# Pool's row transfers in the attention: tied to ScalarE's steps, and the scatter at six a step

## The chip, the cores and the metric

The kernel runs on one core of a Trainium2 chip. The metric is the device time of one execution in microseconds, as the median of several runs. The core's engines each follow their own queue of instructions and meet at semaphores: TensorE (PE), VectorE (DVE), ScalarE (ACT), GpSimd (POOL) and SyncE (SP). Transfers by DMA are issued from SP's, ScalarE's and Pool's queues; only Pool issues those that take their row numbers from a tile (indirect transfers).

## The reference

A "macaron" block on x of 16 x 256 tokens, 128 wide, in float32:

```
x = x + 0.5 * ffn(layernorm(x))
x = x + attention(layernorm(x))        # 16 heads of 64, causal, softmax
x = x + 0.5 * ffn(layernorm(x))

ffn(h): scores = sigmoid(h @ gate_w.T)           # 64 experts
        the best 4 of 8 groups by their two best biased scores; the best 8 experts in them
        weights = scores of the 8 / their sum * 2.5
        y = sum over the 8 experts of weight * (silu(h @ We_gate) * (h @ We_up)) @ We_down
        y + (silu(h @ Ws_gate) * (h @ Ws_up)) @ Ws_down     # shared expert
```

Both feed-forward blocks use the same weights. An expert is 64 wide.

## The kernel before

The 4096 tokens are 8 chunks of 512 (four tiles of 128 tokens each). x stays on the chip in `x_all`. In each feed-forward block four chunks are *dense*: every expert pair is computed for all 512 tokens (33 slots a chunk, lines 824, 828 and 840), and the products are weighted with zero for the experts not chosen; SP spreads the weights (`f_mix_wide`). The other four chunks are *sparse*. Their normalised tokens (`xk`) are written by Pool to rows of the DRAM tensor `x_rows`, sorted by expert: for each of 16 token tiles and each of the 8 choices one indirect transfer of 128 rows (`dispatch`, line 488), 128 transfers in all, each counting `scattered` up by 16. SP then loads groups of four tiles of `x_rows` (`load`, line 742), TensorE turns and multiplies them with the tile's own expert (`quads`: lines 582, 607, 616 and 636), and SP stores the results to `y_rows`. Later Pool fetches for each token tile its 8 lists of result rows (`gather`, line 524, 128 transfers), and VectorE adds them with their weights to `x_all` (line 542).

The program is three blocks of code, one after another on every engine: `ffn_first`, `attention`, `ffn_second`. A block opens when all engines have ended the one before.

`attention` runs 64 steps (16 rows of 256 tokens, four heads a step) and three slots behind them. In slot k TensorE projects q, k and v of step k, while step k-1 goes through the softmax: ScalarE's slot is the exponentials of step k-1 in two pairs (`exp_done` counts pairs), the copies of q (line 1361) and k (line 1377, `k_read`), the three copies of the turned probabilities (line 1386, `probT_done`), then the copy of v. VectorE's slot is the copy of o (line 1496), the normalising of both pairs (lines 1482 and 1487), from time to time the normalising of a row (line 1004), three adds of gathered rows, the maxima of the two pairs (lines 1504, 1505 and 1508; the exponentials wait for line 1508), and between the two maxima up to four steps of the second block's routing, planning and placing. So the attention also holds the gathers and adds of the first block (three lists a step, steps 0 to 42, the add four steps behind its gather) and the front of the second block: the row numbers of its four sparse chunks are placed in steps 48 to 51, and from step 49 on Pool issues half a tile's lists, four transfers, a step. Pool waits in the attention for the row numbers (`idx_done`), for a free buffer before a tile's first gather (`added`), and for the moments of a row before its small pair of instructions that make `rstd` (`rstd_of`, lines 1018 and 1021; `front_rstd`, lines 1557 and 1562). It waits for no step as such.

`ffn_second` starts with the first dense chunk on TensorE, beside it Pool issues what is left of the scatter, now with a small memset behind each transfer (`b.space`, line 143). Then come the sparse groups and then the other three dense chunks. In `quads` the first load waits for all of `scattered`, and so does Pool's first copy of high expert weights (`copy_high`, line 727):

```python
        def load(i):
            if i == 0:
                sp.wait_ge(r.scattered, 16 * TOPK * CT * SPARSE)
            if i >= 3:
                sp.wait_ge(turned, SPARSE + i - 2)
            sp.dma_start(q.xq[:, i % 3, :, :], rows(x_rows, i)).then_inc(loaded[i % 3], 16)
```

The first four groups (`j < SPARSE`) are the shared expert of the sparse chunks and need no load. Ahead of the loads SP's queue has the spreads of the first dense chunk and of the first two groups of the next, and the store of the first dense chunk (`store_x`, line 2102), which waits for that chunk's update of x (line 909).

Of the kernel before, what the change touches and what calls it, by code (L numbers as in the profile page):

```python
# [16 lines left out]
P = 128  # L17
# [4 lines left out]
TOPK = 8  # L22
# [3 lines left out]
H = 16  # L26
HD = 64
SEQ = 256
CT = 4
# [13 lines left out]
SPARSE = 4  # L43
# [8 lines left out]
HALVES = (range(0, TOPK // 2), range(TOPK // 2, TOPK))  # L52
# [96 lines left out]
def router(ctx, nc, tag, order, w, x_all, b, x_rows, f):  # L149
# [13 lines left out]
    idx_done, scattered = sem("idx_done"), sem("scattered")  # L163
# [307 lines left out]
    def on_gpsimd(pool):  # L471
        veps, moments, rstd = b.veps, b.moments, b.rstd

        def rstd_of(r):
            pool.wait_ge(ln_step, LN_STEPS * r.front + 2)
            nc.gpsimd.tensor_tensor(veps[:, :], moments[:, :, 1], w["eps"][:, 0:CT], ALU.add).then_inc(rstd_step, 1)
            pool.wait_ge(rstd_step, 2 * r.front + 1)
            if r.front >= 1:
                pool.wait_ge(ln_step, LN_STEPS * r.front)
            nc.gpsimd.tensor_tensor(rstd[:, :], veps[:, :], w["minus_half"][:, :], ALU.pow).then_inc(rstd_step, 1)  # L480

        def dispatch(i, spaced=True):
            tile, half = divmod(i, 2)
            k, t = divmod(tile, CT)
            if t == 0 and half == 0:
                pool.wait_ge(idx_done, k + 1)
            for j in HALVES[half]:
                nc.gpsimd.indirect_dma_start(  # L488
                    x_rows[:, :], bass.IndirectOffsetOnAxis(ap=b.idx[:, f, CT * k + t, j:j + 1], axis=0),
                    b.xk[:, k, t, :], None).then_inc(scattered, 16)  # L490
                if spaced:
                    b.space(pool)

        return rstd_of, dispatch
# [537 lines left out]

A_ROUTE, A_COUNT, A_PLAN, A_RANK, A_DISPATCH = 14, 44, 45, 48, 49
A_HEAD, A_MIX = 47, 55
GATHER_STEP, ADD_LAG = 3, 4

def attention(nc, w, x_all, banks, psum, rows, b, mix_rows, y_rows, first, second, gathered, added):
# [16 lines left out]
    with ExitStack() as ctx:  # L1055
# [61 lines left out]
        def lists_of(k):  # L1117
            return range(max(GATHER_STEP * k, 0), min(max(GATHER_STEP * (k + 1), 0), SPARSE * CT * TOPK))
# [430 lines left out]
        @block.gpsimd  # L1549
        def _(pool):  # L1550
            rstd_of = rows.on_gpsimd(pool)
            _, dispatch = second.on_gpsimd(pool)
            gather = comb.on_gpsimd(pool)

            def front_rstd(b_):
                pool.wait_ge(c_ln, LN_STEPS * b_ + 2)
                nc.gpsimd.tensor_tensor(b.veps[:, 0:TB], b.moments[:, 0:TB, 1], w["eps"][:, 0:TB], ALU.add)\
                    .then_inc(c_rstd, 1)
                pool.wait_ge(c_rstd, 2 * b_ + 1)
                if b_ >= 1:  # L1560
                    pool.wait_ge(c_ln, LN_STEPS * b_)
                nc.gpsimd.tensor_tensor(b.rstd[:, 0:TB], b.veps[:, 0:TB], w["minus_half"][:, 0:TB], ALU.pow)\
                    .then_inc(c_rstd, 1)

            for k in range(STEPS):
                for i in lists_of(k):
                    gather(i // TOPK, (i % TOPK,), spaced=False)
                if k >= A_DISPATCH:
                    dispatch(k - A_DISPATCH, spaced=False)
                if front_row(k, 6) is not None:  # L1570
                    front_rstd(front_row(k, 6))
                if moments_row(k) is not None:
                    rstd_of(moments_row(k))
# [49 lines left out]
def ffn_first(nc, w, x_all, psum, b, mix_rows, x_rows, y_rows, zero, r, rows, x, dr):  # L1623
# [6 lines left out]
    with ExitStack() as ctx:  # L1630
# [189 lines left out]
        def _(pool):  # L1820
# [35 lines left out]
            for i, slot_ in enumerate(SCATTER_AT):  # L1856
                while waiting and FIRST_AT[waiting[0].n] < slot_:
                    rstd_of(waiting.pop(0))
                if i == 0:
                    pool.wait_ge(zeroed, 16 * len(CLEAR_AT))  # L1860
                dispatch(i)
            copy_high = qd.on_gpsimd(pool)
            pool.wait_ge(dn.x_updated, DENSE)
            for i in range(QUADS_R):
# [76 lines left out]
def ffn_second(nc, w, x_all, psum, b, mix_rows, x_rows, y_rows, r, out, dispatched, gathered, added):  # L1941
# [5 lines left out]
    with ExitStack() as ctx:  # L1947
# [126 lines left out]
        @block.gpsimd  # L2074
        def _(pool):
            rstd_of, dispatch = r.on_gpsimd(pool)
            gather = comb.on_gpsimd(pool)
            for i in range(dispatched, 2 * SPARSE * CT):
                if i == dispatched + 3:
                    rstd_of(in_dense[0])  # L2080
                dispatch(i)
            copy_high = qd.on_gpsimd(pool)
            for i in range(QUADS_R):
                copy_high(i)
                if i == Q_AT + 1 - SPARSE:
                    rstd_of(among)
            for side in range(YBUFS):
                pool.wait_ge(qd.y_stored[side], 16 * len(range(side, QUADS_R, YBUFS)))
            last = (2 * (SECOND_AT[7] - C_FROM)) // 11 + 2
            for t in range(SPARSE * CT):  # L2090
                if t == last:
                    rstd_of(in_dense[1])
                gather(t)
# [30 lines left out]
def macaron(nc, x, P_q, P_k, P_v, P_o, gate_w, gate_bias, We_gate, We_up, We_down, Ws_gate, Ws_up, Ws_down, out):  # L2124
    B, M, _ = x.shape
    tiles = B * M // P
# [8 lines left out]
    with ExitStack() as ctx:  # L2135
# [20 lines left out]
        with ExitStack() as early:  # L2156
# [5 lines left out]
            with nc.sbuf_tensor("zero", [P, CHUNK], F32) as zero:  # L2162
                ffn_first(nc, w, x_all, psum, b, mix_rows, x_rows, y_rows, zero, first, rows, x_v, dr)
            attention(nc, w, x_all, banks, psum, rows, b, mix_rows, y_rows, first, second, gathered, added)
        ffn_second(nc, w, x_all, psum, b, mix_rows, x_rows, y_rows, second, out_v, tiles // (SEQ // P) * (H // 4) - A_DISPATCH,
                   gathered, added)

# [21 lines left out]
```

## Time and profile before

| | |
|---|---|
| median of 3 runs | 1611.32 us (1610.64 to 1612.96) |
| the profiled execution's own time | 1613.64 us |
| its span in the profile | 1611.9 us |
| TensorE busy | 1528.5 us, 95% |
| VectorE busy | 1166.3 us, 72% |
| ScalarE busy | 766.3 us, 48% |
| Pool busy | 722.5 us, 45% |
| scatters, line 488 | 256, 1033 ns each |
| gathers of the attention, line 524 | 128, 977 ns each |

The span is what the hardware profiler recorded on the core; the execution's own time is a little longer. Busy shares are means over stages of different kinds; what bounds a stage is read from the waits in it. In the trace's rows the times are microseconds from the start of the span; a queue's name with a small q (SPq) is the issuing of a transfer, not its data.

### The profile page before, as it was taken

The page shows a single profiled execution, that of the slowest core. Times are in us where ns is not written, and L with a number is a line of the kernel's source. Part 1 is how long each engine was busy: PE and PEld are TensorE (multiplying, and loading weights), DVE is VectorE, ACT ScalarE, POOL GpSimd, SP SyncE. Part 2 cuts the span into 40 slices and gives each one's busy share as a digit, 9 for nine tenths or more (in the row PEclk, how much of TensorE's full clock was granted, in tenths as well). Part 3 has the DMA queues.
Part 4 walks back from the last instruction along what each step waited for, and adds up shares of the span by engine and source line. Part 5 has one row for each costly group of instructions (what it writes and reads, how often), then busy time and mean ns, then how long its engine had stood idle before and what let it go on. Part 6 is the DMA issues. An engine that isn't in the chain of part 4 may idle for free. (4 is left out here: it accounts for less than half of the span.)

```text
span 1611.9 us, 27350 instructions
## 1 busy us (share of the span) xinstructions
PE 1528.5 (95%) x8683; PEld 971.2 (60%) x8683; DVE 1166.3 (72%) x3354; ACT 766.3 (48%) x2105; POOL 722.5 (45%) x1123
## 2 busy tenths in 40 slices
PE   5899999999999899999999998999997999999998
PEld 2344444444788677777777776775446885444443
DVE  4698888765444588989898988765875845768675
ACT  2234223222455577777777776774224552222222
POOL 1000088888222344333334105443883225878730
PEclk9999999999999899999999999999998999999999
DMA  9999655553687111000000001103464884666652
GB/s 184 206 259 249 156 127 140 131 142 93 176 223 206 48 28 28 21 21 21 26 21 24 11 2 38 37 31 92 125 157 135 228 224 112 147 149 146 136 132 65
DMA packets 202043, 181.31 MB, mean 112 GB/s; under 512 B 39408, under 2 KB 154288, under 8 KB 201904
## 3 DMA queue, kind: packets, MB, share of 16 engines
q1 hardware_dynamic: 175056, 132.34, 34.8%
q0 software_dynamic: 16384, 33.59, 7.7%
q10 hardware_dynamic: 10464, 13.63, 2.5%
q8 instruction: 74, 1.21, 0.3%
q14 instruction: 65, 0.53, 0.1%
HBM read 121.83 MB, written 57.67 MB: 111 GB/s over the span
## 5 line engine op out<-in xcount | busy, mean ns | idle before, releaser
L868 ACT ACTIVATE f_hid<-banks 128x512 f32<-128x512 f32 (+1 forms) x264 | 157.6, 597 | 511.6 <-PE banks L828 511.5
L488 POOL DMA_INDIRECT x_rows<-r_xk,r_idx x256 | 264.4, 1033 | 138.6 <-issue 53.3
L890 DVE TENSOR_TENSOR f_hid<-banks,f_hid 128x512 f32<-128x512 f32 (+1 forms) x264 | 181.5, 687 | 145.1 <-ACT f_hid L868 144.9
L840 PE MATMUL banks<-f_hid,wd 128*128 128x512 f32 x528 | 273.3, 601 | 12.5 <-DVE f_hid L903 12.5
L824 PE MATMUL banks<-r_xT_d,gu 128*128 128x512 f32 x528 | 276.4, 605 | 4.7 <-DMA wd<-in_L_ffn_We_down 3.1
L828 PE MATMUL banks<-r_xT_d,gu 128*128 128x512 f32 x528 | 273.5, 600 | 0.0
L903 DVE TENSOR_TENSOR f_hid<-f_mix_wide,f_hid 128x512 f32<-128x512 f32 x256 | 176.0, 687 | 31.9 <-DMA f_mix_wide<-mix_rows 29.5
L840 PEld LDWEIGHTS banks<-f_hid,wd 128*128 128x128 f32 x528 | 99.6, 192 | 146.3 <-issue 120.9
L828 PEld LDWEIGHTS banks<-r_xT_d,gu 128*128 128x128 f32 x528 | 100.8, 191 | 130.1 <-issue 126.5
L824 PEld LDWEIGHTS banks<-r_xT_d,gu 128*128 128x128 f32 x528 | 97.5, 192 | 120.3 <-issue 110.6
L524 POOL DMA_INDIRECT a_g<-y_rows,r_idx x128 | 125.1, 977 | 66.3 <-issue 35.2
L1386 ACT COPY a_probT<-banks 128x512 f32<-128x512 f32 x192 | 106.2, 588 | 101.9 <-PE banks L1249 101.0
L524 POOL DMA_INDIRECT f_g<-y_rows,r_idx x128 | 128.9, 1007 | 41.2 <-issue 20.2
L1487 DVE TENSOR_SCALAR a_prob<-a_prob,a_inv 128x128 f32<-128x128 f32 (+1 forms) x512 | 130.8, 323 | 4.5
L1351 ACT ACTIVATE a_prob<-banks,a_bias 128x256 f32<-128x256 f32 x256 | 127.7, 499 | 0.0
L1228 PE MATMUL banks<-a_kT,a_qT 64*128 64x128 f32 (+1 forms) x1024 | 119.3, 351 | 0.0
L1348 ACT ACTIVATE a_prob<-banks,a_bias 128x128 f32<-128x128 f32 x256 | 99.6, 389 | 30.6 <-DVE a_bias L1508 30.5
L1249 PE MATMUL banks<-ident,a_prob 128*128 128x128 f32 x768 | 106.1, 275 | 2.5 <-ACT a_qT L1361 2.1
L143 POOL MEMSET r_spare<- 128x256 f32 x324 | 106.6, 329 | 0.2
L1264 PE MATMUL banks<-a_probT,a_v 128*64 128x256 f32 (+1 forms) x1024 | 97.3, 332 | 1.5 <-ACT a_probT L1386 0.3
L1249 PEld LDWEIGHTS banks<-ident,a_prob 128*128 128x128 f32 x768 | 89.4, 142 | 12.4 <-issue 3.5
L1504 DVE TENSOR_REDUCE a_top<-banks 128x2 f32<-128x256 f32 x128 | 53.4, 417 | 59.2 <-PE banks L1232 58.4
(243 smaller groups left out, 2879.5 us busy)
## 6 DMA issues: line engine op xcount, KB each, us to landing
f_mix_wide<-mix_rows SPq DMA_DIRECT2D x124, 512.0 KB
x_rows<-zero ACTq DMA_DIRECT2D x12, 1024.0 KB, 5.9
f1q_xq<-x_rows SPq DMA_DIRECT2D x48, 256.0 KB, 3.2
y_rows<-f1q_yq SPq DMA_DIRECT2D x48, 256.0 KB, 2.5
f2q_xq<-x_rows SPq DMA_DIRECT2D x48, 256.0 KB, 3.4
y_rows<-f2q_yq SPq DMA_DIRECT2D x48, 256.0 KB, 2.8
x_rows<-r_xk,r_idx POOLq DMA_INDIRECT x256
wd<-in_L_ffn_We_down SPq DMA_DIRECT2D x7, 512.0 KB, 10.8
```

Of the source, the lines that this page charges most:

```text
L488: nc.gpsimd.indirect_dma_start(x_rows[:, :], bass.IndirectOffsetOnAxis(ap=b.idx[:, f, CT * k + t, j:j + 1], axis=0), b.xk[:, k, t, :], Non ...
L524: nc.gpsimd.indirect_dma_start(g_buf[:, t % GBUFS, j, :], None, y_rows[:, :], bass.IndirectOffsetOnAxis(ap=b.idx[:, f, t, j:j + 1], axis=0 ...
L824: nc.tensor.matmul(gate_bank[g % 3][0:rows, :], w["gu"][:, 0, experts, :].rearrange("p e f -> p (e f)"), x, start=True, stop=True)
L828: nc.tensor.matmul(up_bank[g % 3][0:rows, :], w["gu"][:, 1, experts, :].rearrange("p e f -> p (e f)"), x, start=True, stop=True).then_inc( ...
L840: mm = nc.tensor.matmul(acc[:, :], w["wd"][0:rows, 2 * p, :], d.hid[0:rows, g % HIDS, :], start=(p == 0), stop=(p == PAIRS))
L868: nc.scalar.activation(d.hid[0:rows, g % HIDS, :], gate_bank[g % 3][0:rows, :], ACT.Silu)\
L890: nc.vector.tensor_tensor(d.hid[0:rows, g % HIDS, :], up_bank[g % 3][0:rows, :], d.hid[0:rows, g % HIDS, :], ALU.mult).then_inc(gated, 1)
L903: nc.vector.tensor_tensor(d.hid[:, g % HIDS, :], d.mix_wide[:, n % 2, p % SPREAD, :], d.hid[:, g % HIDS, :], ALU.mult).then_inc(weighted, 1)
L1228: nc.tensor.matmul(scores[pair][h][:, cols], qT[side_rows, i, pair, rows_q], kT[side_rows, i, pair, cols_k], start=(cols.start == 0), stop ...
L1249: mm = nc.tensor.transpose(bank[:, j * P:(j + 1) * P], prob[:, n * P:(n + 1) * P], w["ident"][:, :])
L1351: e = nc.scalar.activation(prob[:, o + P:o + NPB], scores[pair][h][:, P:NPB], ACT.Exp, bias=bias[:, i, pair, 1, h:h + 1], scale=HD ** -0.5 ...
L1487: m = nc.vector.tensor_scalar(prob[:, a:b], prob[:, a:b], inv[:, i, pair, late, h:h + 1], None, ALU.mult)
```

## The change

The unit of `dispatch` becomes one list (one transfer) instead of half a tile. In the attention, each step of Pool gets three points, and Pool waits at each of them for a place in ScalarE's work (`reach`, from step 1 on): at the first for the first pair's exponentials of step k-1, at the second for the copy of k of step k, at the third for the last probability copy of step k-1. Behind each point it issues one gather (steps 0 to 42) or two scatter transfers (from step 49 on). The scatter thus has six transfers a step, 90 in the attention's 15 steps instead of 60, and `ffn_second` begins at list 90 with 38 left, where it had 68. The small `rstd` instructions stay behind the step's transfers. The order of the 128 transfers, the spacing memset outside the attention and the place of `rstd_of` after twelve transfers in `ffn_second` stay as they were. The first block's calls are rewritten for the new unit and do the same.

```diff
-        def dispatch(i, spaced=True):
-            tile, half = divmod(i, 2)
-            k, t = divmod(tile, CT)
-            if t == 0 and half == 0:
-                pool.wait_ge(idx_done, k + 1)
-            for j in HALVES[half]:
+        def dispatch(lists, spaced=True):
+            for i in lists:
+                tile, j = divmod(i, TOPK)
+                k, t = divmod(tile, CT)
+                if t == 0 and j == 0:
+                    pool.wait_ge(idx_done, k + 1)
                 nc.gpsimd.indirect_dma_start(
...
-GATHER_STEP, ADD_LAG = 3, 4
+GATHER_STEP, SCATTER_STEP, ADD_LAG = 3, 6, 4
...
+            def reach(k, part):
+                if k < 1:
+                    return
+                if part == 0:
+                    pool.wait_ge(exp_done, 2 * k - 1)
+                elif part == 1:
+                    pool.wait_ge(k_read, k + 1)
+                else:
+                    pool.wait_ge(probT_done, 3 * k)
+
             for k in range(STEPS):
-                for i in lists_of(k):
-                    gather(i // TOPK, (i % TOPK,), spaced=False)
-                if k >= A_DISPATCH:
-                    dispatch(k - A_DISPATCH, spaced=False)
+                fetched = lists_of(k)
+                for part in range(GATHER_STEP):
+                    reach(k, part)
+                    for i in fetched[part:part + 1]:
+                        gather(i // TOPK, (i % TOPK,), spaced=False)
+                    if k >= A_DISPATCH:
+                        m = SCATTER_STEP * (k - A_DISPATCH) + 2 * part
+                        dispatch(range(m, m + 2), spaced=False)
...
-            for i in range(dispatched, 2 * SPARSE * CT):
-                if i == dispatched + 3:
-                    rstd_of(in_dense[0])
-                dispatch(i)
+            dispatch(range(dispatched, dispatched + 12))
+            rstd_of(in_dense[0])
+            dispatch(range(dispatched + 12, TOPK * SPARSE * CT))
```

## Rows read from the trace of the kernel before

**Rows 1.** The page's chain that ended last, shares of the span by line.
```profile
PE banks L824 5%; PE banks L828 5%; PE banks L840 5%; POOL x_rows L488 4%; PE banks L607 3%; PE banks L636 2%; PE banks L582 2%; POOL r_spare L143 1%; PE banks L616 1%; DVE f_hid L890 0%; DVE f_hid L903 0%; DVE x_all L542 0%; DMA f2q_xq<-x_rows 0%; DMA x_rows<-r_xk,r_idx 0%; DVE x_all L909 0%
```

**Rows 2.** The chain near 1214 us: start, duration, what.
```profile
1213.70 2.28 DMA x_rows<-r_xk,r_idx
...
1215.99 2.92 DMA f2q_xq<-x_rows
```

**Rows 3.** Timeline of Pool: start, duration, what, idle time before it and its releaser.
```profile
1067.30 0.96 POOL L488 DMA_INDIRECT x_rows<-r_xk,r_idx  x1 [0.30 <-issue]
1068.57 0.96 POOL L488 DMA_INDIRECT x_rows<-r_xk,r_idx  x1 [0.30 <-issue]
1110.66 0.96 POOL L488 DMA_INDIRECT x_rows<-r_xk,r_idx  x1 [41.13 <-POOLq L1055]
...
1213.70 0.96 POOL L488 DMA_INDIRECT x_rows<-r_xk,r_idx  x1 [0.17 <-issue]
```

**Rows 4.** Timeline of TensorE around the first loaded group.
```profile
1208.80 0.71 PE L636 MATMUL banks<-wd,f2q_hidT 64*128 64x128 f32 x8
1218.95 1.11 PE L582 MATMUL banks<-ident,f2q_xq 128*128 128x128 f32 x4 [9.44 <-DMA f2q_xq<-x_rows]
...
1223.29 1.11 PE L582 MATMUL banks<-ident,f2q_xq 128*128 128x128 f32 x4
...
1226.18 0.66 PE L582 MATMUL banks<-ident,f2q_xq 128*128 128x128 f32 x4
...
1228.52 0.66 PE L582 MATMUL banks<-ident,f2q_xq 128*128 128x128 f32 x4
```

**Rows 5.** Windows: length, busy PE, PEld, DVE, ACT, POOL, granted clock, DMA share, GB/s.
```profile
1204.00:1206.00 2.00, 1.76 (x16) 1.53 (x15) 0.83 (x2) 1.24 (x3) 1.83 (x4) 1.00 1.00 274
...
1218.00:1220.00 2.00, 1.05 (x5) 1.05 (x6) 0.00 (x0) 0.00 (x0) 1.10 (x5) 0.50 1.00 287
```

**Rows 6.** Windows of whole steps, line 1508 alone: length, DVE busy, count, clock, DMA.
```profile
635.41:778.46 143.05, 5.89 (x32) 1.00 0.09 23
1000.98:1068.07 67.09, 3.29 (x16) 1.00 0.14 43
1068.07:1101.80 33.73, 1.36 (x8) 1.00 0.02 6
```

**Rows 7.** Line 1508, all of it: ns least/median/most; who waited (us, times).
```profile
L1508 DVE TENSOR_SCALAR a_bias<-a_top x128: 169/170/405, 537.7 to 1099.9; 128x4 f32<-128x4 f32 x128
...
  ACT a_prob L1348: 30.5, 21
```

**Rows 8.** Timeline of SP's queue.
```profile
1204.26 0.37 SPq L2102 DMA_DIRECT2D out<-x_all  x1
```

**Rows 9.** Tile f2q_xq, 1200 to 1240 us: its loads.
```profile
DMA to landing us min/median/max: 2.7/3.0/4.3
```

**Rows 10.** Timelines of Pool, ScalarE and VectorE in steps 55 to 57.
```profile
1028.07 0.19 POOL L1018 TENSOR_TENSOR n_veps<-n_moments,eps 128x2 f32<-128x2 f32 x1 [14.24 <-DVE n_moments L997]
...
1029.25 1.03 POOL L488 DMA_INDIRECT x_rows<-r_xk,r_idx  x1 [0.20 <-issue]
...
1029.51 1.07 ACT L1386 COPY a_probT<-banks 128x512 f32<-128x512 f32 x2 [1.03 <-PE banks L1249]
...
1044.20 0.58 DVE L1004 TENSOR_SCALAR n_xn<-x_all,n_moments,n_rstd 128x128 f32<-128x128 f32 x2
```

**Rows 11.** Windows of the same whole steps, line 1487 alone.
```profile
635.41:778.46 143.05, 32.51 (x129) 1.00 0.09 23
1000.98:1068.07 67.09, 16.51 (x64) 1.00 0.14 43
1068.07:1101.80 33.73, 8.09 (x33) 1.00 0.02 6
```

**Rows 12.** Timelines of ScalarE and VectorE in step 57.
```profile
1040.91 0.24 ACT L1351 ACTIVATION_READ_ACCUMULATOR a_prob<-banks,a_bias 128x1 f32 x1
...
1042.04 1.05 DVE L1487 TENSOR_SCALAR a_prob<-a_prob,a_inv 128x128 f32<-128x128 f32 x4
```

More of the change, by code:

```diff
@@ L1860, in _ @@
                     pool.wait_ge(zeroed, 16 * len(CLEAR_AT))
-                dispatch(i)
+                dispatch(range(4 * i, 4 * i + 4))
             copy_high = qd.on_gpsimd(pool)
@@ L2077, in _ @@
             gather = comb.on_gpsimd(pool)
-            for i in range(dispatched, 2 * SPARSE * CT):
-                if i == dispatched + 3:
-                    rstd_of(in_dense[0])
-                dispatch(i)
+            dispatch(range(dispatched, dispatched + 12))
+            rstd_of(in_dense[0])
+            dispatch(range(dispatched + 12, TOPK * SPARSE * CT))
             copy_high = qd.on_gpsimd(pool)
@@ L2164, in macaron @@
             attention(nc, w, x_all, banks, psum, rows, b, mix_rows, y_rows, first, second, gathered, added)
-        ffn_second(nc, w, x_all, psum, b, mix_rows, x_rows, y_rows, second, out_v, tiles // (SEQ // P) * (H // 4) - A_DISPATCH,
+        ffn_second(nc, w, x_all, psum, b, mix_rows, x_rows, y_rows, second, out_v, SCATTER_STEP * (tiles // (SEQ // P) * (H // 4) - A_DISPATCH),
                    gathered, added)
```

## The prediction

> **What bounds the kernel now.** I read four views: the page's chain of work that ended last, then that chain inside the start of the second sparse block, then the timelines of TensorE, SP and Pool around the place it named, and last the attention in stretches of whole steps.
>
> The chain is mostly TensorE, but 4% of the span is Pool's scatter line and 1% the memset that spaces the transfers [rows 1]: a place where TensorE is not the bound. There the chain runs along Pool's scatters to the last one at 1213.70, then 2.28 us until the last one has landed, then 2.92 us for the first load of the scattered rows [rows 2]. Pool's own queue shows how it came to that: in the attention its last transfer starts at 1068.57; then it idles for 41.13 us until the next block of code opens, issues the rest from 1110.66 on, and is done with the last at 1213.70 + 0.96 = 1214.66 [rows 3]. TensorE has finished the first dense chunk and the four shared-expert groups at 1208.80 + 0.71 = 1209.51 and waits 9.44 us for the load [rows 4]. It then starts at the lower clock level: the granted clock of that stretch is 0.50 of 2.4 GHz, after 9 us in which it did nothing [rows 5]. Groups of four tiles start at 1218.95, 1223.29, 1226.18 and 1228.52 [rows 4], that is 4.34, 2.89, then 2.34 us; 2.34 is the pace that the later ones keep. So the late scatter costs 9.44 + (4.34 - 2.34) + (2.89 - 2.34) = **12.0 us** of the end. From the first group on TensorE sets the pace, and what follows is laid out by group and slot: a gain here is carried to the end.
>
> In the attention no single engine sets all steps. Two instructions of line 1508 are one step, so the three stretches are 16, 8 and 4 steps [rows 6]: 143.05/16 = 8.94 us with gathers and the first block's adds, 67.09/8 = 8.39 us while Pool issues scatters nearly without a break, 33.73/4 = 8.43 us with Pool idle. In the first kind VectorE has a part: ScalarE waited 30.5 us in 21 places for line 1508 [rows 7].
>
> **Scatter six a step.** 15 steps (49 to 63) issue 6 instead of 4 transfers: 90 instead of 60, and 38 instead of 68 stay for the second block. The 68 and one pair of small instructions took 1214.66 - 1110.66 = 104.0 us [rows 3]; with some 1.4 us for that pair, 102.6/68 = 1.51 us each. 38 take 57.4 + 1.4 = 59 us: done at about 1169.5, landed 2.3 us later, 45 us earlier than before and 38 us before TensorE wants the rows. That wait is gone.
>
> What is late next: the first load. On SP it stands behind the store of the first dense chunk, issued at 1204.26 in 0.37 us when that chunk's update has ended [rows 8]. The load can be issued at 1204.7. Such loads land after 2.7 to 4.3 us [rows 9]: at 1207.4 to 1209.0. TensorE is ready at 1209.51, so it has 0.5 to 2.1 us in hand. I take no rest of the stall, and no drop of the clock, since TensorE has work until then. If the store, in a stretch where the DMA engines are already fully busy [rows 5], takes 1 us more than the 4.3, the rest is 0.5 us; both ends go into the range as 0 to 1.5.
>
> Cost in the attention: 6 transfers at 1.27 us (the pace of the attention's last two [rows 3]) are 7.6 us of an 8.4 us step; a pair of rstd instructions each fourth step, 1.2 us from its start to the next transfer [rows 10], makes it 7.9 on average. If a step falls behind, the next wait is already met and Pool catches up, because the thresholds only rise. The last pair goes out in step 63, and three more slots of the loop follow before the block closes. The four extra steps filled (60 to 63) are no dearer by the rows: 8.39 us with Pool busy against 8.43 with it idle [rows 6]. Price 0; the ends are below, with the hold.
>
> **Three points per step.** Before, only the small rstd instructions held Pool; transfers ran in bursts. Now step k's first transfer waits for the first pair's exponentials, the second for ScalarE's copy of k, the third for the last probability copy. Three things can come of it.
>
> (a) Later gathers. A tile's last gather goes at the first point of step f+3 at the latest, its first add is in step f+4: over 8 us for a transfer of 1 us plus some 2.3 us to land. Nothing waits. The wait for a free buffer, which Pool met in bursts, is met two steps ahead. Price 0; behind a late gather VectorE would hold all maxima and so ScalarE, but one step of cover would first have to be lost.
>
> (b) Later rstd. The small pair is queued behind step k's third point and its transfers. Before it ran as soon as the moments were there. In step 55 it started at 1028.07, and its reader, line 1004, ran at 1044.20 [rows 10]. The third point of that step is the end of the probability copies at 1029.51 + 1.07 = 1030.6 [rows 10]; two transfers add 2.5, the pair 1.2: 1034.3, with 10 us in hand. Price 0.
>
> (c) Contention between Pool's transfers and VectorE. Line 1487 (eight a step) took 32.51/129 = 252 ns each with gathers, 16.51/64 = 258 with scatters and 8.09/33 = 245 with Pool idle [rows 11]; line 1508 5.89/32 = 184, 3.29/16 = 206 and 1.36/8 = 170 [rows 6], at most 405 [rows 7]. With gathers that is 8 x 7 + 2 x 14 = 84 ns a step, 3.6 us over the 43 gather steps. The new points move this. In step 57 the first pair's exponentials end at 1040.91 + 0.24 = 1041.15; a transfer from there ends near 1042.15, and line 1487 starts at 1042.04, after copying o [rows 12]: an overlap of 0.1 us. The other two I place from the order of the code alone: after the copy of k VectorE is ending its second group of 1487, and after the last probability copy it is in the maxima or in routing, where most of its instructions are of other kinds. So single gathers mostly miss the sensitive instructions, and I take 0.7 us of the 3.6 back. Bounds: all back, -3.6; or one collision a step at line 1508's worst, 43 x (405 - 170) ns = +10.1. The nearest rows, eight steps full of scatters at the same 8.4 us, speak for a value near zero.
>
> A rule of the Trainium skill ("SBUF — State Buffer", Who interferes with whom) speaks against this edit: a tensor_scalar in its two-port mode and a GpSimd instruction exclude each other for the whole instruction, and the one that comes second stands still. The first point puts a transfer just ahead of line 1487. By that rule the sum would be the 1618 us of the lock rival below; [rows 6, 11] show only 7 to 36 ns of it per instruction, and by them it is 1598.6.
>
> **Sum.** Against the profiled execution: 1613.64 - 12.0 - 0.7 = 1600.9. That execution lies 2.3 us above the median of the runs, so 1611.3 - 12.7 = **1598.6 us**.
>
> **Rivals.**
> - *Lock.* Each of VectorE's groups of 1487 that starts just behind a transfer loses half of its 0.95 us. Of 43 gather steps all have one such start: 43 x 0.45 = 19 us, and it is slower than before: 1598.6 + 19 = 1618. For it: the point is fixed relative to VectorE's work, so a hit would be repeated each step, and in steps where VectorE is behind (21 waits of ScalarE) it counts in full. Against: the mean of 258 ns under solid scatters. It decides from 12.7 us on, 0.3 us a step. Chance 0.10.
> - *The load is late anyway.* SP's load, store and the spread before them collide at 1204 to 1206, the load lands at 1211, TensorE waits 2 us and starts again at the lower clock, for up to 2.5 us more: 1598.6 + 4.5 = 1603. For it: DMA share 1.00 there. Against: 38 us without scatters ahead, and 0.5 us in hand even at 4.3. Chance 0.15.
> - *The hold helps.* All contention goes and VectorE's late steps get shorter: 3.6 us and perhaps as much again, where a short delay also moved a wait: 1592 to 1596. Chance 0.10.
> - *Nothing gained.* The scatters are not the last cause of the 9.44 us; SP or the index lists are. Then 1611. Against: the load is issued 2.3 us after the last scatter starts, and SP had been idle since 1204.6. Chance 0.03.
> - *The forecast*: 1596 to 1602, chance 0.62.
>
> **From these.** Range 1592.5 to 1606: it takes in the forecast, the late load, the hold that helps, and an attention dearer by up to 7 us; it leaves out the rest of the lock's cases, no gain, and unforeseen ones. 0.2% is 3.2 us, about what a measurement can tell from no change. Faster: 0.62 + 0.15 + 0.10 + 0.01 of the lock = 0.88; same 0.05; slower 0.07.
>
> **What the profile after would show.** 90 scatters before the block closes, 38 behind it, ended near 1170; Pool idle from there until the high-weight copies; TensorE's wait of 9.44 gone and clock 1.0 through the first groups, 2.34 us apart from the first loaded one; gathers of the attention three a step, evenly; line 1487 at 245 to 258 ns; steps of 8.9 and 8.4 us as before. The prediction is wrong if line 1487 or 1508 has a new mean in the gather steps, if line 1004 waits for Pool, or if the load lands after TensorE is ready.

## The result, and the profile after

The changed kernel took 1599.68 us (median of 4 runs, 1596.78 to 1600.90), the kernel before beside it 1612.14 (4 runs, 1610.64 to 1615.26): a ratio of 0.9917, 95% interval 0.9896 to 0.9938. Forecast were 1598.6 and a range of 1592.5 to 1606. The profiled execution's span fell from 1611.9 to 1598.2 us.

The page's chain that ended last no longer goes through Pool or a DMA (answers to [rows 1]):

```profile
PE banks L824 6%; PE banks L828 6%; PE banks L840 6%; PE banks L607 3%; PE banks L636 2%; PE banks L582 2%; PE banks L616 1%; DVE f_hid L890 1%; DVE f_hid L903 1%; DVE x_all L542 0%; DVE r_eqt L450 0%; PE banks L188 0%; ACT f_hid L868 0%; PE banks L849 0%; DVE r_chosen L344 0%
```

Pool's timeline (answers to [rows 2, 3]): the attention's last transfer, the first of the 38 behind it, and the first copy of high weights, which waits for all of them:

```profile
1099.98 0.95 POOL L488 DMA_INDIRECT x_rows<-r_xk,r_idx  x1 [0.30 <-issue]
1110.86 0.96 POOL L488 DMA_INDIRECT x_rows<-r_xk,r_idx  x1 [9.93 <-POOLq L1055]
...
1168.41 1.04 POOL L488 DMA_INDIRECT x_rows<-r_xk,r_idx  x1 [0.17 <-issue]
1169.44 0.34 POOL L143 MEMSET r_spare<- 128x256 f32 x1
1176.32 0.52 POOL L727 COPY f2q_wd_high<-wd 128x128 f32 x2 [6.54 <-DMA x_rows<-r_xk,r_idx]
```

TensorE's timeline around the first loaded group (answers to [rows 4]):

```profile
1207.19 0.71 PE L636 MATMUL banks<-wd,f2q_hidT 64*128 64x128 f32 x8
1207.83 0.66 PE L582 MATMUL banks<-ident,f2q_xq 128*128 128x128 f32 x4
...
1210.18 0.66 PE L582 MATMUL banks<-ident,f2q_xq 128*128 128x128 f32 x4
```

The wait of 9.44 us is gone and the groups start 2.34 to 2.35 us apart from the first one. SP's timeline (answers to [rows 8]) shows why the load is in time: the store goes out at 1202.65 and the load right behind it, so 4.8 us pass until TensorE wants its rows, and the loads of 1195 to 1240 us landed in 2.7 to 4.4 us:

```profile
1202.65 0.37 SPq L2115 DMA_DIRECT2D out<-x_all  x1
1203.07 1.67 SPq L742 DMA_DIRECT2D f2q_xq<-x_rows  x3
```

The granted clock of that stretch, in windows (columns as in [rows 5]), stays at 1.00:

```profile
1200.00:1208.00 8.00, 7.08 (x60) 6.00 (x58) 3.81 (x8) 4.52 (x10) 0.00 (x0) 1.00 0.80 198
```

In the attention, windows of the same whole steps for line 1508 (answers to [rows 6]), then for line 1487 (answers to [rows 11]):

```profile
635.62:778.80 143.18, 5.45 (x32) 1.00 0.09 23
1001.18:1068.26 67.08, 2.73 (x16) 1.00 0.16 49
1068.26:1101.99 33.73, 1.36 (x8) 1.00 0.15 48
```

```profile
635.62:778.80 143.18, 32.53 (x130) 1.00 0.09 23
1001.18:1068.26 67.08, 16.40 (x64) 1.00 0.16 49
1068.26:1101.99 33.73, 8.42 (x33) 1.00 0.15 48
```

Line 1508 is at a mean of 170 to 171 ns in all three, where it had 184 and 206 in the first two. Line 1487 is at 250, 256 and 255 ns. The stretches are as long as before to 0.15 us, and from the first to the last of the 64 copies of q (line 1361) it is 560.34 us (533.25 to 1093.59), before 560.28. So the contention at line 1508 went and no step got shorter.

Of the 13.7 us between the two spans, 12.0 are the stall. Nearly all of the rest comes from a place that neither the change nor the forecast touches, the first dense chunk: from its first matmul to line 849 it takes 92.8 us before and 91.0 after, 1.8 less, and it starts 0.2 us later. There TensorE waits 2.78 us for the mixing of the first rank (line 373). TensorE's timeline of the kernel before shows the clock falling behind that wait:

```profile
1168.58 0.44 PE L196 MATMUL banks<-ident,f_mix 128*128 128x128 f32 x2 [2.78 <-DVE f_mix L373]
...
1169.72 1.77 PE L828 MATMUL banks<-r_xT_d,gu 128*128 128x512 f32 x2
1171.28 1.91 PE L840 MATMUL banks<-f_hid,wd 128*128 128x512 f32 x2
```

The same stretch of the changed kernel has the same wait, and the pairs of matmuls behind it stay at 1.02 us:

```profile
1168.67 0.44 PE L196 MATMUL banks<-ident,f_mix 128*128 128x128 f32 x2 [2.78 <-DVE f_mix L373]
...
1170.66 1.02 PE L840 MATMUL banks<-f_hid,wd 128*128 128x512 f32 x2
```

The granted clock from 1170 to 1172 us is 0.50, the lower of its two levels (1.2 GHz), in the one and 1.00 in the other. Behind the same wait it fell in four experiments' profiles (five_spaced, spaced_free, six_free, hit_vector) and not in five (hold_only, three_held, five_held, changed_again, warm_wait); which of the two an execution gets stays open. Over medians the gain is 12.5 us.

### The profile page after: what moved, and what is told of

It reads as the page before. It is cut to its first block and busy times, and to the rows that moved or that the text cites. A ratio compares the mean times of both kernels' runs of the same rounds, so it can differ in the third digit from the quotient of the medians.

```text
span 1598.2 us, 27345 instructions
## 1 busy us (share of the span) xinstructions
PE 1525.0 (95%) x8683; PEld 969.3 (61%) x8683; DVE 1166.0 (73%) x3354; ACT 766.1 (48%) x2105; POOL 715.0 (45%) x1093
## 5 line engine op out<-in xcount | busy, mean ns | idle before, releaser
L524 POOL DMA_INDIRECT f_g<-y_rows,r_idx x128 | 129.3, 1010 | 40.8 <-issue 20.2
L143 POOL MEMSET r_spare<- 128x256 f32 x294 | 96.8, 329 | 0.2
```

Source lines behind the costliest of these rows:

```text
L524: nc.gpsimd.indirect_dma_start(g_buf[:, t % GBUFS, j, :], None, y_rows[:, :], bass.IndirectOffsetOnAxis(ap=b.idx[:, f, t, j:j + 1], axis=0 ...
```

## The experiments

Twelve kernels ran, in three groups of four, each group on one chip (13, 9 and 0). In all three the kernel before took about 1758 us, where it had taken 1612 in the first measurement, whose chip is not recorded. So it is not known whether the chip is what differs or something else between the first measurement and the later ones. Each kernel is compared with the kernel before on its own chip:

| kernel | median us (range) | ratio to before [95%] | before there |
|---|---|---|---|
| hold_only | 1615.95 (1611.67 to 1617.56) | 0.9183 [0.9160, 0.9206] | 1758.92 |
| six_free | 1791.44 (1786.44 to 1792.97) | 1.0182 [1.0156, 1.0208] | 1758.92 |
| five_held | 1609.75 (1607.89 to 1610.24) | 0.9153 [0.9134, 0.9172] | 1758.92 |
| three_held | 1633.67 (1632.45 to 1634.89) | 0.9292 [0.9267, 0.9317] | 1758.92 |
| warm_wait | 1756.51 (1744.09 to 1760.43) | 0.9984 [0.9963, 1.0006] | 1757.62 |
| unspaced | 1792.39 (1782.44 to 1795.32) | 1.0207 [1.0187, 1.0227] | 1757.62 |
| hit_vector | 1635.86 (1631.40 to 1640.14) | 0.9305 [0.9279, 0.9330] | 1757.62 |
| mix_later | 1612.18 (1609.74 to 1615.54) | 0.9179 [0.9161, 0.9198] | 1757.62 |
| changed_again | 1614.94 (1610.94 to 1617.69) | 0.9185 [0.9159, 0.9210] | 1757.63 |
| spaced_free | 1665.83 (1662.85 to 1668.44) | 0.9476 [0.9452, 0.9500] | 1757.63 |
| five_spaced | 1602.65 (1597.86 to 1604.27) | 0.9116 [0.9090, 0.9142] | 1757.63 |
| five_spaced_mix | 1595.10 (1594.78 to 1597.36) | 0.9081 [0.9061, 0.9101] | 1757.63 |

### The two edits apart, and the threshold: hold_only, six_free, three_held, five_held

**hold_only** is the changed kernel with four scatter transfers a step, still held to the points:

```diff
-GATHER_STEP, SCATTER_STEP, ADD_LAG = 3, 6, 4
+GATHER_STEP, SCATTER_STEP, ADD_LAG = 3, 4, 4
+SCATTER_PARTS = (0, 2, 3, 4)
...
-                        m = SCATTER_STEP * (k - A_DISPATCH) + 2 * part
-                        dispatch(range(m, m + 2), spaced=False)
+                        m = SCATTER_STEP * (k - A_DISPATCH)
+                        dispatch(range(m + SCATTER_PARTS[part], m + SCATTER_PARTS[part + 1]), spaced=False)
```

> The three points per step, but four transfers a step as before (two, one, one), so that 68 are left for the second block. My theory (all of the gain is the earlier end of the scatter; the hold is worth nothing): the steps of the attention take 8.9 and 8.4 us, TensorE again waits about 9.4 us for the first load and then runs four tiles in 4.3 and 2.9 us, and the time is that of the kernel before, 1612 within 2 us. Rival (the hold gives part of the gain by sparing VectorE): 1608 or less, with attention steps under 8.9 us.

**three_held** has `SCATTER_STEP` 3 and parts (0, 1, 2, 3), **five_held** 5 and (0, 2, 4, 5). **six_free** is the changed kernel without the points:

```diff
                 for part in range(GATHER_STEP):
-                    reach(k, part)
```

> Six transfers a step without the waits for ScalarE's work: Pool runs ahead as before. My theory: the scatter is as early as in the changed kernel, TensorE does not wait for the first load, 1600 within 2 us, and line 1508 is back at a mean of 184 ns with the gathers, 14 ns over the changed kernel, without a longer step. Rival (the hold matters): 1602 or more, by attention steps over 8.95 us.

> The changed kernel with five transfers a step (two, two, one): 53 are left. My theory is a threshold: 53 x 1.51 + 1.4 = 81.4 us after 1110.8 is 1192, landed some us later and still before the load can be issued at 1203; no wait of TensorE, 1600 within 2 us, the same as with six. Rival (a gain in proportion to the transfers moved): half of it, 1606.

> The changed kernel with three transfers a step (one at each point): 83 are left, 15 more than before. My theory: past the threshold each transfer left costs its 1.51 us in full: 1110.8 + 83 x 1.51 + 1.4 = 1237.5, so TensorE waits 9.4 + 22.7 = 32 us and the time is 1612 + 22.7 = 1635. Rival (something else ended the wait too, such as SP's queue): less than 1630.

The threshold came out as the theory has it. TensorE's timeline, the first groups of loaded rows: of hold_only,

```profile
1222.46 1.11 PE L582 MATMUL banks<-ident,f2q_xq 128*128 128x128 f32 x4 [11.70 <-DMA f2q_xq<-x_rows]
...
1226.80 1.12 PE L582 MATMUL banks<-ident,f2q_xq 128*128 128x128 f32 x4
```

and of three_held:

```profile
1241.35 1.11 PE L582 MATMUL banks<-ident,f2q_xq 128*128 128x128 f32 x4 [33.38 <-DMA f2q_xq<-x_rows]
...
1245.58 0.66 PE L582 MATMUL banks<-ident,f2q_xq 128*128 128x128 f32 x4
```

Three a step wait 33.4 us, four 11.7, five nothing: 15 transfers of 1.46 us are 21.9 us, and the wait moved by 21.7. Behind each, the first group takes 4.23 and 4.34 us instead of 2.34. The medians are less far apart, 17.7 us: hold_only's attention is 1.8 us longer, its second group is slow too, and its trace has a later stretch of 6.8 us (from 1344.1) at a granted clock of 0.50 that three_held's has not.

What was not expected is the attention, where four held transfers a step are 143 us quicker than the same four unheld. In the experiments the unheld transfers hurt. The longest case is six_free, where Pool falls behind and then issues 48 in a row, 40 of them in one step (63.0 us long). Pool's timeline, inside the run and at its end:

```profile
1168.05 1.07 POOL L488 DMA_INDIRECT x_rows<-r_xk,r_idx  x1 [0.30 <-issue]
1169.42 0.96 POOL L488 DMA_INDIRECT x_rows<-r_xk,r_idx  x1 [0.30 <-issue]
...
1218.72 0.96 POOL L488 DMA_INDIRECT x_rows<-r_xk,r_idx  x1 [0.30 <-issue]
```

TensorE, ScalarE and VectorE in the same stretch, one timeline each:

```profile
1194.16 0.61 PE L1232 MATMUL banks<-mask,ident_b 128*128 128x256 bf16 x2
1227.69 2.83 PE L1264 MATMUL banks<-a_probT,a_v 128*64 128x256 f32 x16 [32.92 <-ACT a_v L1369]
```

```profile
1190.83 0.58 ACT L1386 COPY a_probT<-banks 128x512 f32<-128x512 f32 x1 [16.16 <-remote]
1225.13 0.58 ACT L1386 COPY a_probT<-banks 128x512 f32<-128x512 f32 x1 [33.72 <-remote]
```

```profile
1218.83 0.42 DVE L1504 TENSOR_REDUCE a_top<-banks 128x2 f32<-128x256 f32 x1 [49.41 <-remote]
```

```profile
DVE a_top L1504 <- remote: 46.7, 9, 6.1
...
ACT a_probT L1386 <- remote: 44.0, 11, 5.8
```

and almost the same (46.7 in 9 places, 46.6 in 11) in warm_wait, whose attention is that of the kernel before. In the trace of before that the prediction read, with the same runs of transfers 0.30 us apart [rows 3], there is none. In six_free a step with five of a run of nine transfers takes 15.7 us instead of 9.0.

The records differ in one more way. The last 128 scatters land with 16 updates each, 2048 in all. Of these the traces of the first measurement hold 2039 (before) and 2035 (changed), the experiments' only 1657 (three_held), 1383 (hold_only), 1292 (five_held), 1264 (five_spaced), 1043 (changed_again), 825 (warm_wait), 670 (six_free) and 396 (unspaced). They all arrived, since the first load waits for all of them; what is missing is their record. Each timed execution of the changed kernel and of the experiments has the profiler's span beside it. None of them is known to have run without the recording, so it is not shown whether the kernels would lose the same time unrecorded. three_held and five_spaced lose records and no time.

Three expectations fall here: hold_only's, that the hold is worth nothing; six_free's; and five_held's 1600, missed by 9 us though its stall is gone. From step 52 on five_held's steps take 9.2 to 9.7 us (7.6 to 9.1 in the changed kernel's first measurement), where the gather steps (one transfer at a point) are as in the first measurement.

### The restart, the gap, VectorE's points, the mixing: warm_wait, unspaced, hit_vector, mix_later

**warm_wait** is the kernel before with 80 transposes of no use between the shared-expert groups and the wait for the first load, to keep the clock up (the `xT_copied` wait moved ahead of them):

```diff
+            if j == SPARSE and tag == "f2q_":
+                for _ in range(20):
+                    for t in range(CT):
+                        nc.tensor.transpose(A[0][:, t * P:(t + 1) * P], b.xk[:, 0, t, :], w["ident"][:, :])
             if j >= SPARSE:
                 i = j - SPARSE
                 pe.wait_ge(loaded[i % 3], 16 * (i // 3 + 1))
```

> The kernel before, with 80 extra transposes of a tile into a free bank, some 9 us of TensorE work, between the last shared-expert group and the wait for the first load; their result is overwritten. My theory: the load comes when it came, at 1218.9, but TensorE's granted clock stays 1.0 and the first two loaded groups take 2.34 us each instead of 4.34 and 2.89: 2.55 us less, 1609.5. Rival (those two groups are slow because their loads or copies are late, not by the clock): starts 4.3 and 2.9 us apart again and 1612.

TensorE's timeline shows the filling, the rest of the wait and the groups:

```profile
1353.80 8.95 PE L580 MATMUL banks<-ident,r_xk 128*128 128x128 f32 x80
...
1365.31 1.11 PE L586 MATMUL banks<-ident,f2q_xq 128*128 128x128 f32 x4 [2.56 <-DMA f2q_xq<-x_rows]
...
1369.05 0.66 PE L586 MATMUL banks<-ident,f2q_xq 128*128 128x128 f32 x4
```

2.56 us were still empty, and the clock, 1.00 from 1353 to 1364, was 0.71 over the next 2 us and 0.50 over the 2 behind them. The first group takes 3.74 us, and the next starts 2.34 behind it (1371.39): the restart costs 1.40 where it cost 2.55 [rows 4]. So the slow groups do come from the clock, as the sum took it, but this kernel did not keep it up, and its time can't be told from the kernel before: the 1609.5 expected, and the 2.55 us less, were not reached.

**unspaced** is the kernel before without the memset between the second block's 68 transfers:

```diff
-                dispatch(i)
+                dispatch(i, spaced=False)
```

> The kernel before, with the memset behind each scatter transfer of the second block left out; the attention is untouched. My theory: the 68 transfers take 1.27 instead of 1.51 us each, end near 1110.7 + 68 x 1.27 + 1.2 = 1198, before the load can be issued at 1203 to 1205: nearly the whole 12 us are gained with no edit in the attention, 1600 to 1602. Rival (the transfers are then held up elsewhere, by the DMA queue or VectorE, and take as long): 1612.

The transfers take less time (the 68 in 1254.97 to 1348.3, most of them 1.26 us apart) and TensorE waits no more for the load, yet the kernel is 2.1% slower, where 1600 to 1602 was expected. The view of waits over 1250 to 1350 us:

```profile
ACT f_hid L868 <- remote: 41.7, 3, 15.5
...
PE banks L196 <- issue: 26.9, 1, 26.9
```

The same late starts, now in the dense chunk, which takes 129.3 us from its first matmul to line 849 instead of 91.0 in warm_wait. The 0.33 us memset, the only thing left out, is what keeps them out of it.

**hit_vector** moves the three points to where VectorE's sensitive instructions begin:

```diff
                 if part == 0:
-                    pool.wait_ge(exp_done, 2 * k - 1)
+                    pool.wait_ge(inv_done, 2 * k - 1)
                 elif part == 1:
-                    pool.wait_ge(k_read, k + 1)
+                    pool.wait_ge(inv_done, 2 * k)
                 else:
-                    pool.wait_ge(probT_done, 3 * k)
+                    pool.wait_ge(top_step, 2 * k + 1)
```

> The changed kernel with its three points moved onto VectorE's work: the first at the first pair's reciprocals, the second at the second pair's, so that each transfer starts together with line 1487, the third at the maxima's end, just ahead of line 1508. My theory (a transfer costs a VectorE instruction at most the 0.2 us seen, and most steps have cover): line 1487 at 255 to 275 ns, attention steps with gathers up to 0.2 us longer, 1600 to 1607. Rival (lock for the whole instruction): groups of line 1487 0.5 to 0.9 us longer each, steps of 9.5 us or more, 1620 or more.

In each gather step a transfer now starts inside the first group of line 1487 (0.25 us behind its start here), and the second one inside the second group. VectorE's timeline and Pool's, one such place:

```profile
700.20 1.03 DVE L1487 TENSOR_SCALAR a_prob<-a_prob,a_inv 128x128 f32<-128x128 f32 x4
```

```profile
700.45 1.02 POOL L524 DMA_INDIRECT a_g<-y_rows,r_idx  x1 [3.30 <-DVE a_inv L1482]
```

The four instructions take 1.03 us, as much as elsewhere, and so does the whole line in windows of 16 such steps:

```profile
635.00:778.00 143.00, 32.61 (x128) 1.00 0.09 23
```

That is 255 ns each, and the steps are as long as the changed kernel's to 0.1 us. The third transfer starts just behind line 1508, not on it (705.38 after 705.14 + 0.17), so for that line nothing was tried; it stays at 170 ns. The expected 1600 to 1607 was missed by far (1635.86), but what this kernel loses lies in the scatter steps, 10.5 to 13.1 us each, with 34.5 us of "remote" waits at line 1504 from 1000 to 1135 us.

**mix_later** moves the mixing of the first rank's rows one slot back in the second block's plan:

```diff
-                    if g == at + T_ROUTE + 9:
+                    if g == at + T_ROUTE + 10:
                         turn_mix(q_)
...
-                    if g == at + T_ROUTE + 9:
+                    if g == at + T_ROUTE + 10:
                         copy_mixT(q_)
```

> The changed kernel with the turning of the routed weights (line 196) one slot later in the second block, on TensorE and ScalarE alike, aimed at TensorE's 2.78 us wait for line 373 near 1168. My theory: the wait shrinks to 0.2 us, the slots behind it move up, 1597 within 2 us. Rival (the wait comes back a slot later, or the spreads of the next chunk come late, because SP stores the weights later): 1600, the same as the changed kernel.

The wait for line 373 is gone (the weight load of line 196 waits 0.64 us for it, beside running matmuls). From the first matmul of the chunk to line 849 it is 88.47 us (1126.05 to 1214.52). The time missed the expected 1597 by 15 us, since the attention's scatter steps had grown here as well (577.3 us from first to last copy of q).

### What of a run hurts, and a better version: changed_again, spaced_free, five_spaced, five_spaced_mix

**changed_again** is the changed kernel, unaltered.

> The changed kernel, unaltered, on the chip of these runs, since it had no run beside the others. If the kernel before takes about 1758 us here: the attention's scatter steps with six transfers grow to 10 to 12 us as they did in mix_later (some 14 us over the 560.3 us from the first to the last copy of q that both kernels had in the first measurement), the second FFN has no wait for its tokens, and the time is mix_later's 1612.2 plus the 2.8 us of the wait that mix_later took away: about 1615, a ratio near 0.918. If the kernel before takes about 1612 here: 1600, and attention steps of 8.4 us. A third result would mean that the loss in mix_later came from its own edit.

1614.94 as expected. First to last copy of q: 575.3 us, 15 more than in the first measurement, all in steps with pairs of scatters. The held kernels are a dose of such pairs: 560.4 us with none a step (three_held), 562.2 with one (hold_only), 569.1 with two (five_held), 575.3 with three. In hold_only and five_held the clock did not fall in the attention's second step, which is 1.6 us shorter for it; the pairs cost them that much more. Pool's timeline shows the last two of four transfers without a pause (1044.77 to 1049.52), as a point already met lets the next pair follow at once:

```profile
1047.29 0.96 POOL L488 DMA_INDIRECT x_rows<-r_xk,r_idx  x1 [0.30 <-issue]
1048.56 0.96 POOL L488 DMA_INDIRECT x_rows<-r_xk,r_idx  x1 [0.30 <-issue]
```

and ScalarE's the copy of k behind them, which follows the copy of q without a wait elsewhere:

```profile
1048.05 0.65 ACT L1361 COPY a_qT<-banks 128x512 f32<-128x512 f32 x1
1050.51 0.59 ACT L1377 COPY a_kT<-banks 128x512 f32<-128x512 f32 x1 [1.80 <-remote]
```

From the chunk's first matmul to line 849 it is 90.99 us (1126.83 to 1217.82): mix_later's edit is worth 2.5 us there, 2.8 in the medians, which are of two chips.

**spaced_free** is the kernel before with the memset between the attention's transfers and no hold:

```diff
-                    gather(i // TOPK, (i % TOPK,), spaced=False)
+                    gather(i // TOPK, (i % TOPK,), spaced=True)
                 if k >= A_DISPATCH:
-                    dispatch(k - A_DISPATCH, spaced=False)
+                    dispatch(k - A_DISPATCH, spaced=True)
```

> The kernel before with nothing held to the steps, but with the memset that it has between the transfers of the second FFN (0.33 us on Pool) put between those of the attention too, gathers and scatters, four a step as it was. If what hurts where the kernel before takes 1758 is that Pool issues transfers with no gap between them, a gap is enough and their place in the step is not needed: the attention is back to 560 to 565 us from first to last copy of q and the time to 1612 (the second FFN's wait for its tokens stays, as nothing changes there). If what counts is that they come many in a run, whatever the gap, it stays above 1700.

Neither of the two. The attention takes 613.4 us (532.34 to 1145.70) against 706.1 in warm_wait and 560.3: the gap takes back 93 of 146 us, and 53 stay. They lie in the steps with a run (from step 8 on, steps with five or six transfers 10 to 12 us, the two with ten and eleven 13.6 and 16.2), again as "remote" waits, now of at most 3.8 us. So a long run hurts with the gap too, but less for each transfer.

**five_spaced** is five_held with `spaced=True` in the attention's scatters.

> Five scatter transfers a step held to the steps as in five_held (which took 1609.7 where 1600 was expected, with scatter steps of 9.2 to 9.6 us), and the memset between those of a pair. If the 9 us came from the two transfers of a pair with no gap between them: scatter steps of 8.4 us, first to last copy of q 561 to 564 us, time 1600 to 1603. If they came from the number of transfers in a step: 1609 to 1611 again.

**five_spaced_mix** has mix_later's edit as well.

> five_spaced with the mixing of the first rank's rows put ten us later in the second FFN's plan, as in mix_later, which took away a wait of 2.78 us of TensorE for line L373. By the theory of the gap 2.8 us less than five_spaced: 1597 to 1600, faster than the changed kernel on this chip and no slower than its first measurement. By the rival 1607.

five_spaced: 560.7 us from first to last copy of q, 1602.65 us. The scatter steps are at a mean of 8.4 us again, with as many transfers as in five_held, and the whole trace has no "remote" wait. Pool's timeline shows one pair, and the point's wait behind it:

```profile
1040.43 0.96 POOL L488 DMA_INDIRECT x_rows<-r_xk,r_idx  x1 [0.17 <-issue]
1041.40 0.33 POOL L143 MEMSET r_spare<- 128x256 f32 x1
1042.20 0.96 POOL L488 DMA_INDIRECT x_rows<-r_xk,r_idx  x1 [0.48 <-ACT a_prob L1352]
```

five_spaced_mix: 1595.10, a ratio of 0.9877 to changed_again on the same chip (1595.10 / 1614.94, of two medians). Its median is the only one here below both kernels' wherever they were measured, though it had no run under the conditions of the first measurement. Of its 7.5 us below five_spaced, where 2.8 were expected, 4.3 are the stretch from the chunk's first matmul to line 849 (92.75 to 88.45): the wait of 2.75, and the clock that had dropped behind it there. Where the other 3 lie is not shown.

## Why the prediction was right, point by point

- **The stall of 12.0 us.** Right in size and place: the wait, the slow groups and nothing in their stead. The dose (three, four, five a step) bears it out, and warm_wait the clock's part, without giving it back.
- **The 38 transfers.** Forecast done at 1169.5; the last one starts at 1168.41. Right. The last landing came at about 1176, later than the 2.3 us taken, and cost nothing.
- **The first load.** Forecast to be issued at 1204.7 and to land before TensorE wants it with 0.5 to 2.1 us in hand. It went out at 1203.07 with TensorE's need at 1207.83: 4.8 us, 0.4 more than the longest landing seen. The rival of the late load fell, narrowly.
- **The hold's 0.7 us, term (c).** Wrong in size, too small to see: 0.06 us the other way. Line 1508 gave back all its 14 ns, but the copies of q come at the same times, so none of it was on the path. By the prediction's own list it would be wrong if line 1508 had a new mean in the gather steps, and it has one, 170 ns for 184; the other signs did not come, line 1487 kept its 250 ns and line 1004 waited for nothing. That ScalarE waited for line 1508 in 19 places (21 before) was read as proof that VectorE's instructions there are; it isn't. The rival "the hold helps" fell with it.
- **The lock rival.** Fell. hit_vector puts a transfer beside each group of line 1487 in the gather steps, so that later instructions of the group start while it runs, and no such step is longer. The Trainium skill ("SBUF — State Buffer", Who interferes with whom) has a tensor_scalar in its two-port mode and a GpSimd instruction shut each other out for the whole instruction; this case's rows do not agree, with 5 to 13 ns of 245 for line 1487. In the changed kernel itself the first point gives the case that the rival feared: a transfer starts at 643.50, a group of line 1487 at 643.58, and the group takes 1.05 us, where the next one, with no transfer beside it, takes 1.01.
- **Nothing gained.** Fell on this measurement. It came near to true in the experiments for the six a step alone: 1614.94 (six) against 1615.95 (four, on another chip), since what the stall gives back, the pairs without a gap take.
- **What no step of it foresaw.** The price of a run of transfers was taken from [rows 6], 8.39 us a step with Pool busy against 8.43 idle, and that holds for the first measurement alone. In the three later ones the same kernel before pays 146 us for its runs (by warm_wait's attention), and the hold, priced at 0.7 us, is worth 143. The forecast of the time would be off by 16 us there and that of the ratio by 7%. The numbers agree: 706.1 - 575.3 = 130.8 us in the attention and 12.0 for the stall are 142.8, measured 1757.63 - 1614.94 = 142.7.

That the forecast of 12.7 us meets 12.5 so closely is partly luck: the stall is 12.0 of it, the hold's 0.7 is nothing, and what fills its place is no larger than the 1.8 us that the clock alone gives or takes from one execution to the next. It is luck too that the first measurement was made where runs of transfers cost nothing.

**Shown and not shown.** Shown, in the experiments, is that the late starts come with Pool's runs of indirect transfers, end with them, grow with their length (single transfers: nothing; pairs at six a step: 1 us a step on average; 40 in a row: 55 us), shrink with a gap of 0.33 us between transfers, and vanish for short groups with the gap. The semaphore records show what comes late, TensorE's signals. Not shown is what holds them back, nor why the waits with the releaser "issue" stand beside the "remote" ones in unspaced. Why the first measurement does not have it stays open too: the chip, and the recording that keeps nearly all updates there and loses many later, are two candidates, and no run tells them apart.

## What to carry to other kernels

A wait of TensorE on a scattered buffer costs its own length and the slow restart behind it; moving transfers into a stage where Pool has time takes away both, and one step of dose on either side (four, five, six) shows where the threshold is. Let Pool issue indirect transfers in groups of one or two, each group held to a place in another engine's work and with some 0.3 us of other work between its transfers: held so, the attention took as long as in the first measurement (560.7 us against 560.3), where without both it took 706. And measure a kernel more than once, on more than one chip, before taking "free" from one trace: here the same pair of kernels has a ratio of 0.992 in one measurement and 0.918 in another. Where a wait has a releaser that no instruction explains, look at when the semaphore's update stands in the records, and at how many updates are missing.

## What the runs showed of the hardware that was not expected

- Beside runs of indirect transfers issued 1.26 us apart, VectorE and ScalarE waited up to 49.4 us for TensorE's signals (six_free), one of which stands 24.0 us behind its matmul's end; so it was on three chips, and in the first measurement, with the same runs of the kernel before, not at all. The queue of these transfers takes 6.9% of the DMA engines' time over six_free's span.
- The memset of 0.33 us between them brings the price of five a step, held in ones and pairs, from some 9 us over 15 steps to zero, and that of the unheld runs from 146 to 53 us.
- After a wait of 2.56 us the granted clock fell to 0.50 in warm_wait. After one of 2.75 to 2.79 us it fell in five executions and not in six others, at the same place of the code.
- A tensor_scalar on 128x128 float32 takes 245 ns with Pool idle and 250 to 258 ns beside indirect transfers, also where one starts inside each group of four; one on 128x4 stays at 170 ns in the steps with single transfers.
